# The last step of a four-layer convolution kernel rearranged: third-layer taps under the last gathers, the last image's unit and closing products ahead

## What is computed

```python
x = x + _L0_conv_ref(_gn(x), ...)   # 2x2 patches, 8 experts, the best two
x = x + _L1_conv_ref(_gn(x), ...)   # deformable 3x3: 4 corners x 9 taps gathered per point
x = x + _L2_conv_ref(_gn(x), ...)   # encode to 256, 16 long filter, gelu, GLU, layernorm, decode
x = x + _L3_conv_ref(_gn(x), ...)   # depthwise 7x7, layernorm over channels, MLP 32 -> 128 -> 32
return x
```

## Time and profile before

| | us |
|---|---|
| median of 3 runs (1692.82 to 1695.66) | 1694.03 |
| the profiled execution | 1693.94 |
| its span, first to last instruction | 1691.8 |
| POOL busy, 71% of the span | 1201.9 |
| PE busy, 79% of the span | 1341.7 |
| DVE busy, 58% of the span | 979.5 |

### The profile page before, as it was taken

The page is one execution under the profiler, slowest core; times in us unless marked ns, Lnnn a source line. Parts: engine busy times, 40 slices in busy tenths (PEclk is TensorE's granted clock), DMA queues, the critical chain, the costliest instruction groups (busy, mean ns, idle before and its releaser), DMA issues.

```text
span 1691.8 us, 13837 instructions
## 1 busy us (share of the span) xinstructions
PE 1341.7 (79%) x4166; PEld 610.6 (36%) x4166; DVE 979.5 (58%) x1622; ACT 513.7 (30%) x870; POOL 1201.9 (71%) x1316
## 2 busy tenths in 40 slices
PE   7868854999969958879979848789839744898697
PEld 6643322443424323324333313334314211333345
DVE  3455554545663478943753588934532794444785
ACT  1222211323332322243523312243313303243345
POOL 8277777756777777777777777777777777777700
PEclk8988976999979979979989869979969976899899
DMA  6232323422332223322332222322221112322000
GB/s 224 70 86 71 83 66 87 121 77 56 92 90 64 63 58 81 89 74 57 88 97 57 65 57 80 101 65 70 61 76 54 50 51 60 83 64 68 27 10 16
DMA packets 110344, 123.04 MB, mean 73 GB/s; under 512 B 49344, under 2 KB 87360, under 8 KB 109888
## 3 DMA queue, kind: packets, MB, share of 16 engines
q0 software_dynamic: 36864, 75.57, 16.0%
q1 hardware_dynamic: 72544, 43.20, 10.2%
q10 hardware_dynamic: 864, 3.41, 0.6%
HBM read 99.79 MB, written 9.01 MB: 64 GB/s over the span
## 4 chain that ended last, share of the span: by engine, by line
POOL 43%; PE 27%; issue 15%; DVE 8%; DMA 3%; ACT 2%; SPq 0%; DVEq 0%; POOLq 0%; ACTq 0%
POOL gt L1130 43%; PE bank L1978 5%; PE bank L1991 4%; PE bank L1893 3%; PE bank L1903 3%; PE bank L1885 3%; PE bank L1928 2%; DVE rb L1752 2%; PE bank L1814 1%; PE bank L2014 1%; DVE gt L1636 1%; PE bank L2035 1%; PE bank L1961 1%; DVE he L1534 1%; DMA gate_of_token<-cw 1%
## 5 line engine op out<-in xcount | busy, mean ns | idle before, releaser
L1130 POOL DMA_INDIRECT gt<-corner_table,idx x1152 | 1146.9, 996 | 394.4 <-issue 347.9
L1636 DVE TENSOR_TENSOR gt<-gt,bank 128x1152 f32<-128x1152 f32 x128 | 172.8, 1350 | 195.5 <-DMA gt<-corner_table,idx 194.7
L1978 PE MATMUL bank<-u,wk 128*128 128x512 f32 x512 | 242.8, 619 | 8.1 <-DMA u<-sqb 8.1
L1991 PE MATMUL bank<-yg,wts 128*128 128x512 f32 x512 | 232.7, 598 | 3.1 <-DVE rb L1692 3.0
L1893 PE MATMUL bank<-xg,w_sb 128*128 128x512 f32 (+1 forms) x288 | 146.3, 591 | 43.2 <-DVE xg L1525 26.0
L1948 PE MATMUL bank<-cst,sm 128*128 128x128 f32 x384 | 75.4, 311 | 125.6 <-DVE sm L1644 125.4
L1534 DVE SCALAR_TENSOR_TENSOR he<-he,bank 128x512 f32<-128x512 f32 (+1 forms) x144 | 89.9, 626 | 122.9 <-PE bank L1893 119.6
L1752 DVE SCALAR_TENSOR_TENSOR rb<-xp,par,rb 128x1024 f32<-128x1024 f32 x124 | 155.2, 1293 | 0.0
L1221 ACT ACTIVATE he<-bank 128x512 f32<-128x512 f32 (+1 forms) x144 | 79.2, 550 | 229.9 <-PE bank L1885 229.5
L1885 PE MATMUL bank<-xp,w_sb 128*128 128x512 f32 (+1 forms) x288 | 140.8, 571 | 4.6 <-ACT he L1221 4.6
L1903 PE MATMUL bank<-he,w_sb 128*128 128x512 f32 (+1 forms) x288 | 139.8, 568 | 5.7 <-DVE he L1534 5.4
(11 more groups left out here) (232 smaller groups left out, 1379.4 us busy)
## 6 DMA issues: line engine op xcount, KB each, us to landing
gt<-corner_table,idx POOLq DMA_INDIRECT x1152
tb<-gate_of_token SPq DMA_DIRECT2D x56, 256.0 KB, 5.1
u<-sqb SPq DMA_DIRECT2D x48, 128.0 KB, 3.3
corner_table<-tb SPq DMA_DIRECT2D x36, 128.0 KB, 2.8
w_sb<-w ACTq DMA_DIRECT2D x2, 1024.0 KB, 7.7
xp<-xg SPq DMA_DIRECT2D x14, 128.0 KB, 2.8
X<-x SPq DMA_DIRECT2D x1, 1536.0 KB, 14.8
out<-X SPq DMA_DIRECT2D x6, 256.0 KB, 2.2
```

The source lines that it names most:

```text
L1130: pool.indirect_dma_start(gt[:, t % GRING, k].rearrange("p a c -> p (a c)"), None, corners, bass.IndirectOffsetOnAxis(ap=idx[s % 2][:, j, ...
L1636: ch.then(tt(rows, rows, share.unsqueeze(2).to_broadcast([P, 4 * KK, C]), ALU.mult))
L1978: op = mm(psum[b][:, :], wk[:, t, d], u4[:, g, at:at + HALF], start=t == 0, stop=t == JJ - 1 and n > 0)
L1991: op = mm(psum[B2.bank(*name)][:, :], w_glu[:, k, col + d * P:col + (d + 1) * P], yg[:, c % 2, k], start=k == 0, stop=k == NB2 - 1)
```

## The change

It touches the order of the last step and of the tail. In `PL` the entry `cut`, the number of entries of part 3's list (its `l3_head` and taps) that stand inside the last step, goes from 20 to 45, and there is a new place `zfold` at 30.7 for part 4's `l3_head`. The last step's first unit moves earlier (`zahead` 16.7 to 16.2, `zastart` 19.2 to 17.7, `zaend` 26.5 to 25.2), and so does its second (`zchead` 24.5 to 24.2, `zcstart` 25.8 to 25.1, `zcstop` 31.6 to 29.8). `l3_mlp` becomes two parts, `l3_hid` (first products and gelu) and `l3_out` (second products). The tail is laid anew: all PE taps of part 4 stand first, part 3's and part 4's closing stands among and behind the last image's units, and part 5 follows with little between its taps. Fillers (`keep`) go away in `turn`, `l3_sum`, `l3_center` and for parts 3 and 4 in the MLP, and 22 behind the last `dcn` become 8. Part 4's folded window moves from `st` to the room of `w_om`, and its centred values to the room of `bb`, so that they can be written while the last tiles still run. PE's `l2_close` waits for the squares only ahead of the second set of products.

```diff
@@ spread, laid
-l3_mlp=6, l1_conv=8)
+l3_hid=3, l3_out=3, l1_conv=8)
...
-        put(order_l3(FOLDED)[:g("cut")], (g("zaend") + 1, 32))
+        put(order_l3(FOLDED)[:g("cut")], (g("zaend") + .4, g("zcstop"), g("cut") // 2), (g("zcstop"), 32, g("cut") - g("cut") // 2))
+        put([("l3_head", FOLDED + 1)], (g("zfold"), g("zfold") + .1))
@@ order, the tail
-    taps, ends = third[g("cut"):-5], third[-5:]
-    some = [(-.9, "l2_head", last, 2)] + spread(taps, [(-.5, g("b1"), len(taps))])
-    some += [(g("e3") + i * g("d3"), *x) for i, x in enumerate(ends)]
...
+    some = [(-.9, "l2_head", last, 2)] + [(-.8, *x) for x in fourth if x[0] == "pe_tap"]
+    some += spread(third[g("cut"):-6], [(-.7, -.2, len(third) - g("cut") - 6)])
+    some += spread([x for x in fourth if x[0] == "tap"], [(.1, 5.6, K7 * K7 - PE_TAPS[FOLDED + 1])])
     second = sum(order_l2(last, 2, 3), [])
-    some += spread(second, [(0, g("last2"), len(second))])
+    closed_at = [i for i, x in enumerate(second) if x[0] == "l2_close"][0]
+    some += spread(second[:closed_at], [(0, 8, closed_at)])
+    for kind, s, at in (("l3_sum", 0, .5), ("l3_center", 0, 1.7), ("l3_scale", 0, 2.6), ("l3_sum", 1, 5.7),
+                        ("l3_center", 1, 6.1), ("l3_scale", 1, 6.9), ("l3_hid", 0, 8.1), ("l2_close", 0, 8.2),
+                        ("l3_out", 0, 8.3), ("l2_var", 0, 8.5), ("l2_end", 0, 8.6), ("l3_add", 0, 8.7),
+                        ("l3_head", 2, 9), ("l3_hid", 1, 9.1), ("l3_out", 1, 10.4), ("l3_add", 1, 11.4)):
+        some += [(at, *x) for x in second + third + fourth + fifth
+                 if x[0] == kind and (kind.startswith("l2") or x[1] == FOLDED + s)]
+    taps, ends = fifth[1:-6], fifth[-6:]
+    some += spread(taps, [(9.2, 12, len(taps))]) + [(13 + i, *x) for i, x in enumerate(ends)]
@@ turn, dcn
-                if (s, t) == (NS - 1, NT * GI - 1):
-                    keep(4, 12)
...
-                    keep(3, 22)
+                    keep(3, 8)
@@ l2_close on PE
-                pe.wait_ge(S["sq_ready"], (s * 8 + cs[-1] + 1) * NB2)
+                B2.read(pe, "z", s, cs[-1], NB2 - 2)
                 B2.read(pe, "z", s, cs[-1], NB2 - 1)
...
+                    if kind == "sq":
+                        pe.wait_ge(S["sq_ready"], (s * 8 + cs[-1] + 1) * NB2)
```

## The result

The changed kernel takes 1712.58 us (median of 4, 1711.19 to 1716.59) beside 1693.59 us of the kernel before on the same chip: a ratio of 1.0116 (95% interval 1.0103 to 1.0128), slower by 19 us. Forecast were 1703.3, with a range to 1708. The direction was right, the size was not. The profiled execution is the longest of the four, 1716.59 us with a span of 1714.5.

| stretch, us | before | predicted | after |
|---|---|---|---|
| S | 1590.13 | 1599.8 | 1609.86 |
| S to T0 | 14.2 | 18.9 | 19.75 |
| T0 to the end of the strips | 56.5 | 55.7 | 57.3 |
| strips to the last image's tap sum | 17.5 | 13.3 | 14.1 |
| from there to the end of the span | 13.4 | 13.4 | 13.5 |

What follows compares the result with a forecast made beforehand. POOL's gathers took 43% of the span and hid the rest until tile 31, then one chain from S. Terms +9.7 + 4.7 - 0.8 - 4.2 = +9.4 on 1691.8, plus 2.14, gave 1703.3 us; range 1690.5 to 1708.

Steps and rivals of the forecast that it cites:

- S: End of the last `sample` on DVE; predicted at 1599.8, 9.7 us late, with 8.9 of waits on DVE.
- S to T0: PE's 16 taps of part 4 wait for POOL's 24 matrices: 18.9 us, 4.7 more than before.
- T0: Start of the last image's first `l2_y` on PE, at 1604.36 before the change.
- T0 to the end of the strips: The last image's third-layer unit, closing, normalisation and strips under the new PE list: 55.7 us, 0.8 less.
- strips to the last image's tap sum: The last image's 49 taps, 24 on PE and 25 on DVE: 13.3 us, 4.2 less.
- from there to the end of the span: Closing after the last image's tap sum, predicted to stay at 13.4 us.
- 158.6: Way from the pair's first `l2_y` at 1441.2 to S, predicted at 1599.8.
- one trace's head, less 2.7: Head of the last step's pair, claimed to end some 2.7 us sooner, so PE begins at 1441.2 instead of 1446.99.
- the 76.7 us: From the pair's first `l2_y` to its last `l2_z`, nearly all PE work, taken as unchanged by the change.
- My rival of half clock in the first `l2_y`, twice: Half clock in two `l2_y` and behind the 4.5 stall: + 2.5 + 1.7, about 1707.5; chance 0.13.
- The stall: PE waits ahead of part 4's `l3_sum` and `l3_center` for GLU, two `l2_z` and four DVE passes: 4.5 us.
- my 1.7: Added to the last image's taps for a half-clock beginning after PE has idled 7 us.

Runs made afterwards that it cites:

- front_only: The changed kernel's new places of the last step with the tail of the kernel before behind them, removed fillers still out: 1708.14 us, ratio 1.0074.
- rotate: The changed kernel, but POOL makes the 16 matrices that part 4 uses first: 1711.32 us, ratio 1.0094.
- close4_late: The changed kernel with part 4's sum behind the next `l2_g`, its mean square and scale behind the last `l2_z`: 1714.94 us, ratio 1.0120.
- rotate_nofill: The changed kernel with part 4's matrices made first and the 8 fillers behind the last dcn taken out: 1705.40 us, ratio 1.0064.
- cut26: The changed kernel with `cut` 26 instead of 45 (19 taps, not 34, ahead of the last `sample`), part 3's closing later: 1710.73 us, ratio 1.0103.
- cut26_sum: As cut26, against the changed kernel, with part 4's DVE taps beginning behind part 3's sum: 1704.65 us, ratio 1.0069.
- cut26_rotate: The changed kernel with the edits of cut26 and rotate_nofill together: 1710.10 us, ratio 1.0091.
- best26: The changed kernel with fillers in PE's gaps, part 4's matrices first, `cut` 26 and part 4's taps behind part 3's sum: 1698.22 us, ratio 1.0040.
- best31: best26 laid anew: `cut` 31, closings of parts 3 and 4 later, mean square's bank like the mean's: 1688.68 us, ratio 0.9986.

## Why the prediction was wrong in size

**First, S: the step that failed.** I had it as 1441.2 (the pair's first `l2_y`) plus 158.6. Measured were 1447.96 and 161.9, so 6.8 and 3.3 us.

- The beginning, 6.8. I took one trace's head, less 2.7. In the eight profiles of kernels whose lists are alike up to there (after, front_only, rotate, close4_late, rotate_nofill, cut26, cut26_sum, cut26_rotate) it lies between 1440.2 and 1448.0, mean 1444.3; after is the latest. Two things vary in it. One is the gathers: the first of the last 36 issues starts at 1543.0 in after, at 1539.6 before, and between 1537.9 and 1543.5 in the eight, though no gap between two issues of the last step is over 0.4 us. That is 3.4 of the 6.8. The other is the way to the pair. Counted back from that issue, the pair begins 97.8 to 99.1 us ahead in five of the eight, as I had it (98.4), but only 93.9 to 95.1 us ahead in after, front_only and rotate_nofill: the other 3.4. In the ten us that end 110 us ahead of that issue PE's granted clock is 0.50 in these three and 0.72 to 0.80 in the five; in after and in rotate:

```profile
1423.01:1433.01 10.00, 7.67 (x27) 0.50 0.27 80
```

```profile
1417.94:1427.94 10.00, 7.50 (x35) 0.72 0.25 79
```

So this variation goes together with the clock. What sets it so in one execution and not in another stays open. Before, S stood 4.33 us behind the last issue. In the five kernels that are unchanged as far as S it stands 14.3 to 19.4 behind it. I wrote myself that a late DVE costs nothing during the gathers, and didn't draw the other half: once DVE sets S, a late beginning of the pair is in the time.
- The way from there, 3.3. Of that the pair's unit is 1.1, its closing to X 2.0, head and fold -1.2, first tap to S 1.4. The clock is in it. I priced it in the closings (3.5 instead of 1.9). The pair's first `l2_y` stood in the 76.7 us with the 4.86 of before and took 6.14, 1.3 more; and image 3's dcn took 5.30 instead of 2.74, and DVE's wait for it was 6.64 instead of my 4.0. The closing to X is something else: 1.8 of its 2.0 is the root, which I took as before. ACT now copies a turn ahead of it, and waits for that turn behind all the closing products on PE:

```profile
1535.41 0.49 ACT L1277 ACTIVATE st<-bank 128x384 f32<-128x384 f32 x1 [3.37 <-PE bank L1957]
```

My rival of half clock in the first `l2_y`, twice, gave PE's taps spaced by POOL as its reason, so it meant the last image's. There two took 3.60 each, and it did not come true; its other half did, 8.25 instead of 7.0 us behind the stall. Its 1707.5 was too low because S was.

A median run took 4 us less than the profiled one. Against the median, the forecast is 9.3 short.

**Second, S to T0**: right in its mechanism and nearly in size, 19.75 for 18.9. The 24 matrices took 18.56 us instead of 17.84. The two runs on POOL's order bear it out: 17.4 with part 4's matrices first, 14.0 with the fillers out as well.

**Third, T0 to the strips**: 57.3 for 55.7. The stall is as predicted (4.3 for 4.5); behind it two `l2_g` took 8.25 instead of 7.0 us at the lower clock.

**Fourth, the last taps**: 14.1 for 13.3. The first ten took 7.0 us against 4.65 behind fillers (best26), 2.35 for my 1.7.

The sign was right because its reason was right: the list put DVE behind the gathers. The range was too narrow because its upper end kept the gathers and the beginning of the pair's unit fixed.

## What to carry to other kernels

Where a slow stream (here the gathers) hides everything else, slack against it is worth keeping: work moved under it is free only until the engine's list reaches the stream's end later than the stream, and from then on variation upstream that the stream hid shows, too. Price such a move by the whole chain to that point, over several profiles, and take the length of products behind a gap from products behind a gap (here 1.4 to 1.9 times as long). What is made in sequence for several users (the matrices) should be made in the order in which it is needed, and a sum that an in-order engine waits for should stand ahead of all work that is not part of it.

## What was not expected of the hardware

POOL issues gathers more slowly where DVE has more taps beside them. The windows of the last 36 issues (stretch, length, POOL busy with count, granted clock, DMA share, GB/s) in the kernel before, after, and in best31:

```profile
1539.61:1585.80 46.19, 35.52 (x36) 0.82 0.25 66
```

```profile
1543.01:1591.68 48.67, 38.00 (x36) 0.86 0.25 63
```

```profile
1540.75:1586.44 45.69, 35.02 (x36) 0.91 0.18 52
```

With 34 taps ahead of the last `sample` they take 38.0 to 39.0 us (seven profiles), with 19 taps 35.0 to 36.2, with 15 taps 35.5; single issues grew from 0.94 to 2.22 us. It cost nothing here, as DVE was later still. cut26 differs from the changed kernel up to S only in its taps, 15 fewer, and has 36.2 instead of 38.0: that much is the taps'. In the kernel after, the 15 issues that overlap a tap hold 4.0 of the 4.1 us by which the 36 exceed 0.94 each; but before, 12 overlap one, for 0.7 us. How a tap lengthens an issue, and why not each time, stays open. The Trainium skill (SBUF — State Buffer, SBUF: two separate sides) says that VectorE and GpSimd share a port pair which one instruction holds to its end, that a VectorE instruction with two SBUF inputs, as a tap is, takes it only against a GpSimd instruction that reads SBUF, and that a VectorE operation in a two-port mode keeps GpSimd from writing the descriptors of a DMA that it issues. The longer issues under taps agree with a shared port in direction, but no row here shows the lock itself, nor that an issue reads SBUF.
